# Split float32r probabilities and values, streamed q and k weights, and attended rows normalised on GpSimd, in a decoder layer on one core

## The chip, the cores and the metric

The kernel runs on one core of one Trainium2 chip. The metric is device time in microseconds. Before the change it was 2292.56 us, the median of 3 runs (2286.22 to 2292.59).

## What is computed

One decoder layer on x of 8 x 512 x 512 floats (B=8, S=512, D=512). It has three parts; the change lies in the first, the self-attention. It is done for each of the 8 batches:

```python
h = rmsnorm(layernorm(x)) * norm_w
q, k, v = h @ w_q, h @ w_k, h @ w_v            # 16 heads of 64
ll = where(causal, q @ k.T * 64**-0.5, -1e30)   # 512 x 512 a head
scores = h @ scorer_w                           # the 128 best tokens are attended to once more
lg = where(idx <= pos, q @ k[idx].T * 64**-0.5, -1e30)
attn = softmax(concat(ll, lg))
x1 = layernorm(x) + (attn_local @ v + attn_top @ v[idx]) @ w_out
```

A token among the 128 best counts twice, so the kernel doesn't gather: it multiplies the values and the sum's column by `twice` (1 or 2). Behind this part come a cross-attention with a router and a block on the routed tokens; both stay as they are.

## The kernel before

`self_attention` runs a loop over the 8 batches, and in it a plan (`attention_plan`) that every engine follows in the same order, each taking the steps that are its own. Semaphores order the engines among each other; on each engine the order is that of the plan.

A batch is one window of 512 tokens. TensorE first projects v (8 products of 128 tokens by 512 columns; each product is 12 float32r matmuls, as both operands are split into a high and a low float32r part and the low-low term is left out) and the first q and k. The 16 heads go in 8 pairs; a pair has five units u0 to u4, each of which fills a bank of 128 x 512 scores. u0 and u1 are the last 128 queries of either head against 512 keys, u2 and u3 the first 128 queries against 128 keys and the third 128 against 384, u4 the second 128 queries of both heads against 256 keys. So there are 40 units a batch (g or i in the plan, i = 5 p + u). At slot g the plan has, in this order:

- s(g): scores. TensorE adds q times the high part of k, q times the low part (`k_second`), and the causal mask as a bf16 product with the identity (L672 to L676). VectorE takes the negated maximum of each row (L543, L548), ScalarE the exponential into `probs` (L418).
- t(g-2): TensorE transposes the probabilities (L684), VectorE copies them from the bank to `probs_t` (L556).
- ot, only at g = 8, 13, ... (always a u3): TensorE transposes the attended rows of the pair before (L708), for which all five units of that pair must have been divided (`o_copied`). ScalarE copies them to `o_t` (L426).
- pv(g-3): TensorE multiplies the transposed probabilities by the values with a column of `twice` beside them (65 columns, f32, L699), VectorE takes the reciprocal of the sum and multiplies (L570, L571). TensorE's pv(i) needs `o_copied` of unit i-2.
- in u0 the projection of q for the next pair, in u2 that of k (L595 to L597). ScalarE makes the high parts (L405; L408 and L409, four copies of 64 partitions for k), VectorE the low parts (L532 in u1, L536 in u3). The scores of the next pair's u0 wait for both.
- single steps of the next batch: at g=5 its statistics (VectorE L439 to L443, then a chain on GpSimd L338 to L352 that ends in the normalised xb), at g=14 the dot product with the scorer, at g=18, 22, 24, 27, 29 the ranks that give `twice`; from g=40 on the transposes ht of the normalised tokens, between the last units.

The banks of t, ot, ht and score alternate between two: a transposition into a bank waits until the one two before it in this row has been read out (`ts_ready`, `ot_ready`). Score banks, `probs`, `probs_t` and output banks alternate in the same way. At the end of a batch TensorE multiplies `o_t` by `w_out` (out, L723) and VectorE adds the residual.

Ahead of the loop all weights are loaded and split whole: `w_q`, `w_k` and `w_v` come in six pieces of 1 MB through the two halves of `o_t`; ScalarE makes each high part (L381), VectorE each low part (`split`, L494), and pieces 2 to 5 (q and k) lie between the scorer's and the ranks' steps on VectorE. The first copy of v (L396, ScalarE) waits for `twice`.

## Time and profile before

| | |
|---|---|
| median of 3 runs | 2292.56 us |
| profiled execution, its own time | 2291.27 us |
| its span | 2289.5 us |
| mean granted clock of TensorE | 0.947 |
| busy: TensorE matmuls, weight loads | 2122.6 us (93%), 1653.9 us (72%) |
| busy: VectorE, ScalarE, GpSimd | 1340.6 (59%), 843.0 (37%), 429.6 us (19%) |
| pv, L699 (2560 matmul records) | 328.7 us busy, 271 ns each |
| copy of probabilities, VectorE L556 (320) | 217.6 us busy, 680 ns each |

Busy time counts an instruction from its start to its end, and matmuls overlap, so the mean of one is longer than its share of the engine; the distance between starts tells that. The attention's last VectorE operation starts at 1534.83 us, the cross part's first operations at 1538.03. Loads and matmuls of one f32 product are recorded as two passes each, those of float32r as one.

### The profile page before, as it was taken

What the parts mean: (1) busy time and instruction counts of PE and PEld (TensorE: products, weight loads), DVE (VectorE), ACT (ScalarE), POOL (GpSimd) and SP (SyncE); (2) the same over time, 40 slices, a digit from 0 to 9 for tenths busy, and PEclk for the clock granted to TensorE, in tenths of its full rate; (3) what the DMA queues carried; (4) which work ended last, traced back from release to release, by engine and by line L of the source; (5) the groups of instructions that cost most, each with busy time, mean ns of one, the idle gap of its engine ahead of it and who ended that gap; (6) DMA issues with size and microseconds to landing.
All of it is one profiled execution on the core that took longest, in us unless ns stands there. A gap on an engine that the chain in (4) does not pass through costs nothing. (4 is left out here: it accounts for less than half of the span.)

```text
span 2289.5 us, 35705 instructions
## 1 busy us (share of the span) xinstructions
PE 2122.6 (93%) x12029; PEld 1653.9 (72%) x12029; DVE 1340.6 (59%) x3146; ACT 843.0 (37%) x1541; POOL 429.6 (19%) x669
## 2 busy tenths in 40 slices
PE   3999999999999999999999999977899988978899
PEld 2886787688688688678768858846788887854543
DVE  5584376178177358537617817735887878645401
ACT  3442344244144144234424414415444444313210
POOL 2100000010010010000001001015776767420000
PEclk9999999999999999999999999998887979669899
DMA  5000000100100100000010010012023212150000
GB/s 197 1 1 34 28 1 15 47 1 1 61 1 1 61 1 1 33 29 1 15 47 1 1 61 1 1 57 62 27 68 129 62 57 72 38 201 1 0 0 19
DMA packets 47290, 82.33 MB, mean 36 GB/s; under 512 B 10196, under 2 KB 10196, under 8 KB 46602
## 3 DMA queue, kind: packets, MB, share of 16 engines
q1 hardware_dynamic: 46474, 77.95, 10.2%
q8 instruction: 103, 1.69, 0.3%
q0 software_dynamic: 640, 2.10, 0.2%
q14 instruction: 73, 0.60, 0.1%
HBM read 62.20 MB, written 17.83 MB: 35 GB/s over the span
## 5 line engine op out<-in xcount | busy, mean ns | idle before, releaser
L418 ACT ACTIVATE probs<-s_bank,nmax 128x512 f32<-128x512 f32 (+3 forms) x512 | 249.1, 525 | 364.0 <-DVE nmax L548 254.8
L699 PE MATMUL o_bank<-vals,probs_t 128*128 128x65 f32 x2560 | 328.7, 271 | 0.1
L699 PEld LDWEIGHTS o_bank<-vals,probs_t 128*128 128x128 f32 x2560 | 310.8, 192 | 14.9 <-DVE probs_t L556 12.9
L548 DVE TENSOR_REDUCE nmax<-s_bank 128x1 f32<-128x512 f32 (+2 forms) x384 | 184.2, 507 | 185.1 <-PE s_bank L676 182.4
L723 PE MATMUL pj_bank<-w_o,o_t 128*128 128x512 f32 x512 | 221.1, 592 | 0.0
L556 DVE COPY probs_t<-pt_bank 128x512 f32<-128x512 f32 x320 | 217.6, 680 | 0.1
L684 PE MATMUL pt_bank<-ident,probs 128*128 128x128 f32 x1280 | 194.0, 274 | 2.6 <-ACT o_t L426 2.6
L672 PE MATMUL s_bank<-k_twice,q_both 128*128 128x512 f32 (+3 forms) x512 | 189.9, 373 | 1.9 <-DVE k_second L536 1.9
L332 POOL TENSOR_TENSOR idle<-ones 128x4 f32<-128x4 f32 x41 | 10.0, 245 | 959.2 <-DMA probs<-in_x 957.1
L723 PEld LDWEIGHTS pj_bank<-w_o,o_t 128*128 128x128 f32 x512 | 96.6, 190 | 118.6 <-issue 118.6
L532 DVE SCALAR_TENSOR_TENSOR q_both<-pj_bank,q_both 64x512 fp32r<-64x512 f32 x128 | 88.1, 688 | 142.0 <-ACT q_both L405 139.3
L396 ACT ACTIVATE vals<-pj_bank,twice 128x512 f32<-128x512 f32 x64 | 43.9, 687 | 333.2 <-PE pj_bank L597 327.5
L674 PE MATMUL s_bank<-k_second,q_both 128*128 128x512 f32 (+3 forms) x512 | 163.9, 320 | 0.0
L1270 PEld LDWEIGHTS x_o_bank<-vx,p_t 77*128 77x128 f32 x1024 | 147.3, 222 | 16.9 <-issue 7.5
L1270 PE MATMUL x_o_bank<-vx,p_t 77*128 77x33 f32 x1024 | 141.9, 298 | 3.2 <-DVE att L1152 3.2
L684 PEld LDWEIGHTS pt_bank<-ident,probs 128*128 128x128 f32 x1280 | 135.5, 141 | 3.5 <-issue 3.5
L588 DVE TENSOR_TENSOR probs<-pj_bank,probs 128x512 f32<-128x512 f32 x32 | 22.1, 692 | 192.1 <-PE pj_bank L723 179.8
L595 PE MATMUL pj_bank<-wv_hi,ht_hi 128*128 128x512 f32 x256 | 104.6, 409 | 22.5 <-ACT vals L396 9.6
L1256 PE MATMUL e_bank<-qk_bd,xl_t 128*128 128x308 f32 x256 | 99.6, 522 | 23.4 <-DVE e L1134 22.7
L1033 POOL TENSOR_TENSOR e<-e,fill 128x616 f32<-128x616 f32 x64 | 95.3, 1490 | 123.1 <-DVE fill L1140 122.9
L676 PE MATMUL s_bank<-causal_b,ident_b 128*128 128x128 bf16 x512 | 117.8, 230 | 0.0
L405 ACT ACTIVATE q_both<-pj_bank 64x512 fp32r<-64x512 f32 x128 | 75.5, 590 | 88.7 <-PE pj_bank L597 88.0
(263 smaller groups left out, 4202.1 us busy)
## 6 DMA issues: line engine op xcount, KB each, us to landing
xb<-in_x SPq DMA_DIRECT2D x9, 1024.0 KB, 5.7
xt<-x SPq DMA_DIRECT2D x36, 256.0 KB, 3.0
probs<-in_x SPq DMA_DIRECT2D x32, 256.0 KB, 2.7
x<-probs SPq DMA_DIRECT2D x32, 256.0 KB, 2.0
am<-in_L_ffn_attention_mask SPq DMA_DIRECT2D x8, 1024.0 KB, 5.2
out<-x SPq DMA_DIRECT2D x32, 256.0 KB, 2.1
w_sb<-in_L_ffn_w SPq DMA_DIRECT2D x2, 4096.0 KB, 20.3
o_t<-in_L_attn_w_v SPq DMA_DIRECT2D x2, 1024.0 KB, 9.7
```

The lines of the kernel that those rows point to most:

```text
L418: ins = nc.scalar.activation(probs[:, i % 2, c0:c0 + nk], s_bank[i % 2][:, c0:c0 + nk], ACT.Exp, bias=nmax[:, i % 4, n:n + 1])
L548: ins = nc.vector.tensor_reduce(nmax[:, i % 4, n:n + 1], s_bank[i % 2][:, c0:c0 + nk], AX.X, ALU.max, negate=True)
L556: nc.vector.tensor_copy(probs_t[:, i % 2, :], pt_bank[slot][:, :]).then_inc(ts_ready, 1)
L595: nc.tensor.matmul(out, lhs_hi, rhs_hi, start=start, stop=False)
L672: nc.tensor.matmul(s_bank[slot][:, c0:c0 + nk], queries, k_twice[:, p % 2, h, 0:nk], start=True, stop=False)
L674: nc.tensor.matmul(s_bank[slot][:, c0:c0 + nk], queries, k_second[:, p % 2, h, 0:nk], start=False, stop=False)
L676: ins = nc.tensor.matmul(s_bank[slot][:, c0 + nk - P:c0 + nk], ident_b[:, :], causal_b[:, :], start=False, stop=True)
L684: ins = nc.tensor.transpose(pt_bank[slot][:, P * j:P * j + P], probs[:, i % 2, P * j:P * j + P], ident[:, :])
L699: ins = nc.tensor.matmul(o_bank[slot][:, o0:o0 + VW], probs_t[:, i % 2, c0 + P * kt:c0 + P * kt + P], vals[:, kt, 2 * p + h, :], start=(kt ...
L723: ins = nc.tensor.matmul(pj_bank[slot][:, :], o_t[:, c, P * i:P * i + P], w_o[:, c, :], start=(c == 0), stop=(c == NPAIR - 1))
L1256: ins = nc.tensor.matmul(e_bank[:, c, 0:CH * SK], xl_t[:, (i // 2) % 2, P * k:P * k + P], qk_bd[:, n.par, k].rearrange("p h k -> p (h k)") ...
L1270: ins = nc.tensor.matmul(o_bank[:, VX * h:VX * h + VX], p_t[:, i % 2, h // CH, P * (h % CH):P * (h % CH) + P], vx[:, n.par, 2 * CH * (i % ...
```

## The change

- pv: ScalarE copies the transposed probabilities to a float32r high part `pt_hi`, VectorE subtracts it from the bank for a low part `pt_lo`. The values are split too: columns 0 to 63 low, 64 to 127 high, and two columns of `twice`. TensorE multiplies `pt_hi` by all 130 columns and `pt_lo` by the 66 of the high part and the sum.
- the attended rows: ScalarE copies the bank to `o_part`, GpSimd adds low and high halves, raises the sum to the power -1 and multiplies. TensorE's pv(i) waits for that copy (`part_ready`) of unit i-2, ScalarE's copy for `o_copied` of unit i-2.
- q and k weights: no longer held whole. Each pair's 128 columns are loaded again in each batch into one of two buffers (SP, behind the projection that used the buffer); ScalarE makes the high part, GpSimd the low part, at the plan's new steps wq and wk (u3 and u4; in pair 0 at g = 1 to 4).
- ScalarE takes t(g-2) ahead of s(g). The causal mask and its identity are float32r instead of bf16. The self-attention's semaphores are cleared and a barrier follows it.

```diff
+WQ_AT = (1, *range(3, UNITS * (NPAIR - 1), UNITS))
+WK_AT = (2, *range(4, UNITS * (NPAIR - 1), UNITS))
...
+            def split_qk(b, n, i):
+                pl.wait_ge(wqk_hi_ready[n], b * NPAIR + i + 1)
+                nc.gpsimd.tensor_tensor(wqk_lo[:, i % 2, "qk".index(n)], wqk_raw[:, i % 2, "qk".index(n)],
+                                        wqk_hi[:, i % 2, "qk".index(n)].bitcast(F32),
+                                        ALU.subtract).then_inc(wqk_ready[n], 1)
...
+                    if kind == "pv":
+                        part = o_part[:, i % 2, 0:n, :]
+                        pl.wait_ge(part_ready, b * NU + i + 1)
+                        nc.gpsimd.tensor_tensor(part[:, :, 0:HD], part[:, :, 0:HD], part[:, :, HD:2 * HD],
+                                                ALU.add).then_inc(sum_ready, 1)
+                        step(nc.gpsimd.tensor_tensor(part[:, :, 2 * HD], part[:, :, 2 * HD], minus[:, 0:n], ALU.pow))
+                        pl.wait_ge(sum_ready, b * NU + i + 1)
+                        if u == 0 and p >= 1:
+                            pl.wait_ge(pt_ready, pt(b, ("ot", p - 1))[1])
+                        nc.gpsimd.tensor_tensor(dst, part[:, :, 0:HD],
+                                                part[:, :, 2 * HD:2 * HD + 1].broadcast_to((P, n, HD)),
+                                                ALU.mult).then_inc(o_copied, 1)
+                    if kind in ("wq", "wk"):
+                        split_qk(b, kind[1], i + 2)
...
+                    if kind == "t":
+                        slot, ready = pt(b, (kind, i))
+                        act.wait_ge(pt_ready, ready)
+                        if i >= 2:
+                            act.wait_ge(pv_ready, b * NU + i - 1)
+                        nc.scalar.copy(pt_hi[:, i % 2, :], pt_bank[slot][:, :]).then_inc(pt_hi_ready, 1)
+                    if kind == "pv":
+                        act.wait_ge(pv_ready, b * NU + i + 1)
+                        if i >= 2:
+                            act.wait_ge(o_copied, b * NU + i - 1)
+                        nc.scalar.copy(o_part[:, i % 2, 0:n, :],
+                                       o_bank[i % 2][:, 0:n * VW].rearrange("p (n v) -> p n v", n=n)
+                                       ).then_inc(part_ready, 1)
...
                     if kind == "t":
-                        nc.vector.tensor_copy(probs_t[:, i % 2, :], pt_bank[slot][:, :]).then_inc(ts_ready, 1)
-                    if kind == "pv":
-                        step(nc.vector.reciprocal(o_rden[:, i % 2, 0:n], src[:, :, HD]))
-                        nc.vector.tensor_tensor(dst, src[:, :, 0:HD],
-                                                o_rden[:, i % 2, 0:n].unsqueeze(2).broadcast_to((P, n, HD)),
-                                                ALU.mult).then_inc(o_copied, 1)
+                        dv.wait_ge(pt_hi_ready, b * NU + i + 1)
+                        nc.vector.tensor_tensor(pt_lo[:, i % 2, :], pt_bank[slot][:, :],
+                                                pt_hi[:, i % 2, :].bitcast(F32), ALU.subtract).then_inc(ts_ready, 1)
...
+                                nc.tensor.matmul(o_bank[slot][:, o0:o0 + VW], pt_hi[:, i % 2, keys],
+                                                 vals[:, kt, 2 * p + h, :], start=(kt == 0), stop=False)
+                                ins = nc.tensor.matmul(o_bank[slot][:, o0 + HD:o0 + VW], pt_lo[:, i % 2, keys],
+                                                       vals[:, kt, 2 * p + h, HD:VW], start=False, stop=last)
```

VectorE's splits of the q and k weights ahead of the loop (`split(2)` to `split(5)`) go, and it gains the low part of v, one operation for each product of v, with `v_ready` behind it.

## Rows read from the trace of the kernel before

**Rows 1.** Stretches: length, busy PE, PEld, DVE, ACT, POOL; clock, DMA share, GB/s.
```profile
50.00:55.00 5.00, 4.63 (x11) 3.67 (x12) 0.00 (x0) 0.90 (x2) 0.00 (x0) 0.52 0.05 16
500.00:550.00 50.00, 49.45 (x346) 42.62 (x345) 40.40 (x99) 23.94 (x46) 0.00 (x0) 1.00 0.00 1
```

**Rows 2.** Timeline of TensorE in batch 1: start, duration, operation, count.
```profile
269.73 0.22 PE L672 MATMUL s_bank<-k_twice,q_both 128*128 128x128 f32 x1
...
285.50 0.22 PE L672 MATMUL s_bank<-k_twice,q_both 128*128 128x128 f32 x1
...
286.66 0.60 PE L708 MATMUL pt_bank<-ident,o_norm 128*128 128x128 f32 x4
...
290.08 0.49 PE L672 MATMUL s_bank<-k_twice,q_both 128*128 128x512 f32 x1
...
291.32 1.11 PE L699 MATMUL o_bank<-vals,probs_t 128*128 128x65 f32 x8
292.23 0.48 PE L595 MATMUL pj_bank<-ht_hi,wq_hi 128*128 128x512 f32 x1
...
295.07 0.39 PE L672 MATMUL s_bank<-k_twice,q_both 128*128 128x512 f32 x1
```

**Rows 3.** Timeline of VectorE in the same stretch.
```profile
286.42 0.75 DVE L548 TENSOR_REDUCE nmax<-s_bank 128x1 f32<-128x128 f32 x2 [1.88 <-PE s_bank L676]
287.09 0.68 DVE L556 COPY probs_t<-pt_bank 128x512 f32<-128x512 f32 x1
...
288.42 0.23 DVE L571 TENSOR_TENSOR o_norm<-o_bank,o_rden 128x64 f32<-128x64 f32 x1
288.56 1.38 DVE L536 TENSOR_TENSOR k_second<-pj_bank,k_twice 64x512 fp32r<-64x512 f32 x2
...
290.58 0.68 DVE L556 COPY probs_t<-pt_bank 128x512 f32<-128x512 f32 x1
```

**Rows 4.** Groups by line and shape: busy us, mean ns; idle time before, its releasers.
```profile
L699 PEld LDWEIGHTS o_bank<-vals,probs_t 128*128 128x128 f32 x2560 | 310.8, 192 | 14.9 <-DVE probs_t L556 12.9
...
L674 PEld LDWEIGHTS s_bank<-k_second,q_both 128*128 128x128 f32 x512 | 97.7, 191 | 4.7
...
L676 PEld LDWEIGHTS s_bank<-causal_b,ident_b 128*128 128x128 bf16 x512 | 49.2, 96 | 59.8 <-issue 54.2
...
L1022 POOL TENSOR_TENSOR scales<-scales,x_half 128x1 f32<-128x1 f32 x32 | 20.5, 641 | 2.5
```

**Rows 5.** Timeline of the start: last split on VectorE, TensorE's wait.
```profile
47.08 2.28 DVE L494 TENSOR_TENSOR wk_lo<-o_t,wk_hi 128x2048 fp32r<-128x2048 f32 x1
...
50.37 0.80 PE L595 MATMUL pj_bank<-wv_hi,ht_hi 128*128 128x512 f32 x1 [9.65 <-ACT vals L396]
```

**Rows 6.** Timeline of ScalarE in the stretch of rows 2.
```profile
285.70 0.58 ACT L408 CAST k_twice<-pj_bank 64x512 fp32r<-64x512 f32 x1 [1.21 <-PE pj_bank L597]
...
288.08 0.84 ACT L418 ACTIVATE probs<-s_bank,nmax 128x128 f32<-128x128 f32 x2
288.81 0.59 ACT L426 COPY o_t<-pt_bank 128x512 f32<-128x512 f32 x1
```

**Rows 7.** Timeline of GpSimd: the statistics of the next batch.
```profile
279.83 0.20 POOL L338 TENSOR_TENSOR st<-mv,eps_ln 128x4 f32<-128x4 f32 x1 [53.61 <-DVE mv L443]
280.11 1.01 POOL L339 TENSOR_TENSOR st<-st,half 128x4 f32<-128x4 f32 x1
...
284.84 3.02 POOL L352 TENSOR_SCALAR xb<-xb,st 128x512 f32<-128x512 f32 x4
```

**Rows 8.** One line's instructions: ns min/median/max, first and last start.
```profile
L1042 POOL TENSOR_TENSOR x<-xt,att x64: 714/730/1179, 1578.4 to 1987.7; 128x256 f32<-128x256 f32 x64
```

**Rows 9.** Timeline of TensorE at the end of a batch.
```profile
386.99 1.11 PE L699 MATMUL o_bank<-vals,probs_t 128*128 128x65 f32 x8
387.94 0.61 PE L623 MATMUL pt_bank<-ident,xb 128*128 128x128 f32 x4
389.09 0.65 PE L708 MATMUL pt_bank<-ident,o_norm 128*128 128x128 f32 x4 [0.55 <-DVE o_norm L571]
```

More of the change, by code:

```diff
@@ L42 @@
 NU = NPAIR * UNITS
-VW = HD + 1
+VW = 2 * HD + 2
 class Tally:
@@ L116, in attention_plan, with transposes_first @@
             plan.append(("ht", g - NU))
+        if g in WQ_AT:
+            plan.append(("wq", WQ_AT.index(g)))
+        if g in WK_AT:
+            plan.append(("wk", WK_AT.index(g)))
     plan += [("out", t) for t in range(TT)]
     return plan
+def transposes_first(plan):
+    order = list(plan)
+    for n in range(len(order) - 1):
+        if order[n][0] == "s" and order[n + 1][0] == "t":
+            order[n], order[n + 1] = order[n + 1], order[n]
+    return order
 def bank_index(plan, kinds):
@@ L192, in self_attention @@
         pj_ready, row_copied = sem("pj_ready"), sem("row_copied")
-        v_ready, v_sum_ready, qk_hi, qk_lo = sem("v_ready"), sem("v_sum_ready"), sem("qk_hi"), sem("qk_lo")
+        v_hi_ready, v_ready, v_sum_ready, qk_hi, qk_lo = (
+            sem(n) for n in ("v_hi_ready", "v_ready", "v_sum_ready", "qk_hi", "qk_lo"))
+        wqk_in = {n: [sem(f"w{n}_in{i}") for i in range(2)] for n in "qk"}
+        wqk_hi_ready = {n: sem(f"w{n}_hi_ready") for n in "qk"}
+        wqk_ready = {n: sem(f"w{n}_ready") for n in "qk"}
         s_ready = sem("s_ready")
@@ L272, in _, with next_weights @@
             sp.wait_ge(sw_out, 16)
+            def next_weights(b):
+                for i in range(NPAIR):
+                    for n in "qk":
+                        sp.wait_ge(pj_ready, pj(b, (n, i))[1])
+                        load_qk(n, (i + 2) % NPAIR)
             def results(b):
@@ L299, in _ @@
                 sp.wait_ge(half_done, 16 * B * TT // 2 + 1)
+            for n in "qk":
+                for half_in in wqk_in[n]:
+                    sp.wait_ge(half_in, 16 * (B * NPAIR // 2 + 1))
         @block.gpsimd
@@ L353, in stats @@
                                             ALU.mult, ALU.add).then_inc(h_ready, 1)
+            def split_qk(b, n, i):
[3 more added lines that the diff above has]
+                                        ALU.subtract).then_inc(wqk_ready[n], 1)
             stats(0)
-            with pl.Fori(0, B) as b, done.loop(b, 14 + TT, B):
+            for i in range(2):
+                for n in "qk":
+                    split_qk(0, n, i)
+            with pl.Fori(0, B) as b, done.loop(b, 14 + TT + NU, B):
                 for r in range(2):
```

176 lines of the change are left out of this document (100 added, 76 removed).

## The prediction

> **What bounds the kernel now.** I read the page first, then the stretches, then the timelines of one stretch engine by engine. The page says that TensorE works through nearly all of the span and that the self-attention fills the first 1535 us of it; only that part is edited. The stretches show a steady one: TensorE is busy 49.45 of 50 us, VectorE 40.40, ScalarE 23.94, GpSimd 0.00, at full clock [rows 1]. So GpSimd is free and VectorE is the second busiest, but a busy TensorE only says that it sets the pace, not that nobody makes it wait. For that I read the timeline of a pair's stretch [rows 2]. A pair of heads has five units u0 to u4; in each slot TensorE does s (scores), t (transposes of the unit two slots earlier) and pv (of three slots earlier), and in u0 and u2 a q or k projection. From s(u3) at 285.50 to the q projection at 292.23 there is no projection: 6.73 us. Nearly all of it is back to back; the starts of s(u0) and pv(u2) alone are late, and they stand right behind VectorE's rows: k_second ends at 289.94 and s(u0) starts at 290.08, the copy of unit u2 ends at 291.26 and pv(u2) starts at 291.32 [rows 2, 3]. TensorE's own work is therefore the floor, and what waits cost is read in this stretch.
>
> **TensorE's work stays.** pv has 8 f32 passes a unit now, and 8 float32r matmuls after (4 high of 130 columns, 4 low of 66). The weight load is 192 ns a pass in f32 and 191 ns in float32r [rows 4], and the eight passes of pv(u2) take 0.91 us, 291.32 to 292.23 [rows 2], 0.114 each; as the loads are alike, I let the load set the pace of both. I take 0 for the swap; ends: -0.04 us a pass (2560 passes, -105 us) if float32r loads could hide, +0 otherwise, near the row of equal loads. The causal matmul loses its short bf16 load (96 against 191 ns, 512 times: at most +49 us). But the loader stands idle for 59.8 us in all before these loads, 54.2 of it at issue, and for 4.7 before as many float32r loads [rows 4]: at most -55 us. The two are alike; I take 0.
>
> **Start.** Four splits of q and k weights leave VectorE, 2.29 us each, the last at 47.08 [rows 5]; the v block on TensorE waits 9.65 us for work behind them, until 50.37 [rows 5]. 50.37 - 4 x 2.29 + 0.75 for the new low part of v = 42.0: -8.4 us. The long idle time had also let the granted clock fall: it is 0.52 from 50 to 55 us, where eleven matmuls run at half speed [rows 1]. About 2 us come back if the idle time is only 1.5 us. Start: **-10 us**. The small loads and splits that come instead (ScalarE 4 x 0.59, GpSimd 4 x 1.2) lie beside the first v block.
>
> **The prices of what is moved.** ScalarE: copy of the transposed probabilities 0.59, as the 128x512 copy at 288.81 [rows 6]; copy of the attended rows 0.3 (130 columns) or 0.4 (260), under that 0.59; split of weights 0.6 for q and k, once a pair. VectorE: the copy of 0.68 becomes a subtraction of about the same length (k_second: 1.38 for two [rows 3]); reciprocal and multiplication leave. GpSimd has no row of these shapes: 4 elements of a two-input operation take 0.20 [rows 7], 256 take 0.73 in the median and 1.18 at most [rows 8], so 64 or 128 take 0.4 or 0.5; a power takes 0.64 for one element [rows 4] and 1.01 for four [rows 7], so 0.6 or 0.7; dependent steps stand 0.08 apart (280.03 to 280.11 [rows 7]). One unit: 0.4+0.6+0.4+0.1 = **1.5** (u0, u1) or 0.5+0.7+0.5+0.16 = **1.86** (u2 to u4); bounds 1.0 and 2.6. A weight split of 512 columns: 1.2 (0.73 to 1.46). The Trainium skill (GPSIMD Engine Reference, Engine selection) speaks against this move: it puts a two-input elementwise operation on GpSimd at about twice VectorE's time. By its ratio of 1.96 and the 0.23 us of VectorE's 64-element multiplication [rows 3] such an operation would take 0.45 instead of 0.4, an estimate from that page, and the sum below would be some 2 us higher.
>
> **The walk through a pair (0 = start of s(u3)).** Check on before: k copies on ScalarE end at 2.56, k_second runs 3.06 to 4.44, s(u0) starts 4.58, pv(u2) 5.82, q 6.73 [rows 2, 3, 6]. After: the copies of k still end at 2.56, and only then ScalarE makes the high part of u1, to 3.15; its low part on VectorE 3.2 to 3.9. k_second slides behind it, 3.9 to 5.3. t(u2) on TensorE uses the bank of t(u1), free at 3.9 instead of 2.3: it starts at 3.95, 0.8 us after s(u4) is through. pv(u1) follows without a gap; s(u0) waits for k_second until 5.35. On ScalarE come exponential 0.73, o_t 0.59, attended rows 0.3, weight split 0.6, and the high part of u2 ends at 6.0; its low part at 6.7; pv(u2) starts at 6.75 and q at 7.65. That is **+0.93 us a pair**; the slots with q and k projections (2.84 us each, 292.23 to 295.07 [rows 2]) take up the rest. Four pairs of a batch (stretches behind k of pairs 3 to 6) go like this: +3.7 us. Bounds 0.3 and 1.6 a pair.
>
> **The queue behind the statistics.** GpSimd does the next batch's statistics at g=5, a chain of steps from 279.83 to 287.86, 8.03 us [rows 7]. Now it does nothing else; after the change pv(3) and pv(4) of pair 0 are queued behind it. The transposes ot(0) on TensorE (g=8) need all five units of pair 0. Counted from s(u3) of pair 0 (269.73), VectorE's statistics are ready at 10.1 now and, with the first stretch 1.4 us longer (one more weight split lies in it) and the low parts, at 12.7; GpSimd ends them at 20.7, pv(3) and pv(4) at 24.5. ot(0) starts at 16.93 now [rows 2], and TensorE, 2 us later by these two, would reach it at 18.9: it stands for 5.6 us, and what is queued behind it (pv(5), s, t) with it. In the stretch behind, everyone has caught up, -0.5. Sum **+7.1 us a batch**; bounds 3 (GpSimd at its cheap prices) and 9. TensorE idles long enough there that its clock may fall: it was 0.52 after the 9.65 us at the start, full after the waits of under 1 us elsewhere [rows 1, 5]. Cost 0 or about 2.2 us; I take **+1.1**.
>
> **The pair without projections and the tail.** Behind k of the last pair no projection gives time back: the walk continued loses 1.25 us up to the next u2. Then ot(6) waits for pv of unit 34: ScalarE has it copied 1.1 us behind its end, GpSimd adds 1.86, while only s and t lie between: **+1.8**. At the end ot(7) starts at 389.09, 1.15 us after pv(39) is through and the ht transposes behind it begin (387.94 [rows 9]); after, the ScalarE copy (0.45) and GpSimd with the unit before still in its queue (2.4) come between: **+1.7**. VectorE's relief takes away about -0.5 a batch, where score and ranks made TensorE wait. The longer way of v through VectorE (0.75 us) lies within the next projection of 2.84 us and costs nothing; uncovered it would be 8 x 0.75 us a batch.
>
> **Sum.** A batch: 7.1 + 1.1 + 3.7 + 1.25 + 1.8 + 1.7 - 0.5 = 16.1; eight: +129. Start -10. The added clearing of semaphores and barrier between attention and cross part: +1 (0 to 5). Total +120. The profiled execution took 2291.27 us (span 2289.5), 1.3 under the median of the runs, so **2411 us**, by either.
>
> **Rivals.**
> 1. The statistics queue costs little (GpSimd's steps at 0.2 to 0.3 us, the stats reached earlier), pairs cost as walked: 129 - 8 x 7 = 73, less 10: 2354. For: GpSimd's rows for these shapes are missing. Against: even at 1.0 us a unit, pv(4) ends later than TensorE gets to ot(0).
> 2. Faster. The float32r passes of pv run under the row that I went by: the loads hide and a pass takes some 0.07 us. It decides from about 0.05 us less a pass, since 2560 passes must pay for 120 us. At 0.07 with half of the walked waits: 2291 - 105 + 65 - 10 = 2241; at half the effect 2285. For: a float32r matmul is one pass, an f32 one two. Against: the load rows of 191 and 192 ns.
> 3. Slower still: GpSimd shares its way to memory with VectorE's two-input operations, and a unit takes 2.6 us; then it is later than TensorE in every pair's ot, about 1.5 us each, and in the tail: +80, 2490. For: the 256-element operation takes up to 1.18 us in the cross part [rows 8], where both are busy. Against: the VectorE operations here read one operand from a bank of TensorE's.
>
> **Chances.** Forecast (2370 to 2450) 0.54, rival 1 (2320 to 2370) 0.20, rival 3 0.10, rival 2 0.12, all covered and no change 0.04. 0.3% (7 us) is about what a measurement can tell here: faster 0.12, same 0.04, slower 0.84. The range leaves out rival 2, no change and the upper end of rival 3: 2320 to 2475.
>
> **What would show it.** Right: in the changed trace, per batch one wait of 4 to 7 us of TensorE at the ot transposes of pair 0, released by GpSimd; s(u3) to q about 7.6 us in later pairs, with t(u2) waiting for the low part; pv at 0.9 us for eight; ot(7) about 3 us after pv(39). VectorE under 1300 us busy, ScalarE about 1200, GpSimd about 1000. Wrong: pv clearly under 0.8 us, no wait at ot, or stretches that keep 6.7 us; then TensorE's floor moved or the queues cover more than walked.

## The result and the profile after

The changed kernel takes 2467.16 us in the median (2454.63 to 2476.08, 4 runs), the kernel before 2290.5 us beside it: ratio 1.077, 95% interval 1.0717 to 1.0823. It is slower, as forecast, and the time lies within the range given (2320 to 2475 us), but above the 2370 to 2450 us that had the largest chance, and 56 us above the 2411 us predicted. The profiled execution of the changed kernel took 2454.63 us (span 2452.9), 163 us more than the profiled one of before, which took 2291.27 us (span 2289.5).

Busy times of the changed kernel, from the page's first part and its row of the granted clock in 40 slices; below them its span and mean granted clock:

```profile
PE 2204.3 (90%) x12029; PEld 1761.0 (72%) x12029; DVE 1311.1 (53%) x2566; ACT 1139.9 (46%) x2309; POOL 1048.3 (43%) x1762
...
PEclk9899989999899998999999989998888788858999
...
core 0: 2452.9 us, clock 0.919
```

GpSimd went from 429.6 to 1048.3 us, ScalarE from 843.0 to 1139.9, VectorE from 1340.6 to 1311.1, and no engine but TensorE is near its span. The new thing is the clock: 0.919 in the mean, where before had 0.947. At full clock a share of 1 is 2.4 GHz and at half 1.2 GHz, so a mean of 0.919 over 2452.9 us is 2 x 0.081 x 2452.9 = 397 us at half clock; before it was 2 x 0.053 x 2289.5 = 243 us, nearly all behind the attention. The change added some 150 us of half clock.

Where it begins is seen in the first batch. The same engine's rows in stretches of the changed kernel (start:end, length, busy time and count of TensorE, its weight loads, VectorE, ScalarE, GpSimd, then the granted clock):

```profile
50.00:55.00 5.00, 5.00 (x23) 4.14 (x23) 1.50 (x2) 1.38 (x2) 0.00 (x0) 1.00 0.01 3
...
88.00:99.00 11.00, 7.05 (x50) 6.33 (x48) 6.90 (x14) 7.20 (x15) 9.66 (x22) 0.98 0.16 48
99.00:109.00 10.00, 9.62 (x45) 9.43 (x45) 2.65 (x4) 4.66 (x10) 5.04 (x9) 0.50 0.01 2
109.00:114.00 5.00, 5.00 (x18) 4.01 (x18) 0.11 (x1) 0.73 (x2) 1.53 (x3) 0.67 0.00 0
150.00:200.00 50.00, 48.02 (x333) 42.82 (x331) 35.83 (x67) 37.32 (x81) 26.90 (x50) 1.00 0.11 33
```

The half clock of the start is gone: 1.00 in 50 to 55 us, against 0.52 [rows 1]. From 99 to 109 us the clock is 0.50. TensorE's timeline and GpSimd's tell why (start, duration, engine, line, operands, count; in brackets the idle time just before and who ended it). First TensorE:

```profile
99.38 1.11 PE L806 MATMUL pt_bank<-ident,o_norm 128*128 128x128 f32 x4 [4.33 <-POOL o_norm L441]
100.14 0.46 PE L796 MATMUL o_bank<-vals,pt_hi 128*128 128x130 f32 x1
...
109.12 0.77 PE L690 MATMUL pj_bank<-ht_hi,wqk_hi 128*128 128x512 f32 x1
...
113.45 0.40 PE L767 MATMUL s_bank<-k_twice,q_both 128*128 128x512 f32 x1
```

Then GpSimd:

```profile
88.16 0.20 POOL L389 TENSOR_TENSOR st<-mv,eps_ln 128x4 f32<-128x4 f32 x1 [0.48 <-DVE mv L550]
...
93.18 3.02 POOL L403 TENSOR_SCALAR xb<-xb,st 128x512 f32<-128x512 f32 x4
96.17 0.46 POOL L435 TENSOR_TENSOR o_part<-o_part 128x128 f32<-128x128 f32 x1
96.58 0.71 POOL L437 TENSOR_TENSOR o_part<-o_part,minus 128x2 f32<-128x2 f32 x1
97.36 0.40 POOL L441 TENSOR_TENSOR o_norm<-o_part 128x128 f32<-128x128 f32 x1
...
98.92 0.40 POOL L441 TENSOR_TENSOR o_norm<-o_part 128x128 f32<-128x128 f32 x1
```

GpSimd does the next batch's statistics from 88.16 to 96.2, 8.0 us as in [rows 7], then the units 3 and 4 of pair 0; only with the last, at 99.3, may TensorE do ot(0). It has stood for 4.33 us, and behind that wait the next 10 us run at half clock: a pv of eight matmuls starts at 100.14 and the next s at 101.85, 1.71 us where it is 0.89 elsewhere. The q projection that starts at 109.12 takes 4.33 us instead of 2.84, and during it the clock comes back.

Not every batch goes like this. TensorE at ot(0) in the second batch and in the fourth:

```profile
308.35 1.11 PE L806 MATMUL pt_bank<-ident,o_norm 128*128 128x128 f32 x4 [4.29 <-POOL o_norm L441]
...
722.21 0.66 PE L806 MATMUL pt_bank<-ident,o_norm 128*128 128x128 f32 x4 [1.13 <-POOL o_norm L441]
```

In batches 1, 2, 5 and 7 the wait is 4.27 to 4.33 us, and 13.7 us at half clock go with it. In batches 3, 4, 6 and 8 the clock has been at half for 6.8 us one stretch earlier (in the fourth from 706.2 to 713.1 us), so TensorE comes to ot(0) later, waits 1.11 to 1.58 us, and no half clock follows. The waits ahead of that earlier fall (1.12 and 0.29 us, between k(1) and q(2)) are the same in all eight batches; why the clock falls there in only four of them is not shown.

A later pair, at full clock, is where the walk of the prediction can be checked. Timeline of all engines, changed kernel, from s(u3) to the next q:

```profile
173.94 0.22 PE L767 MATMUL s_bank<-k_twice,q_both 128*128 128x128 f32 x1
...
175.91 0.58 ACT L500 CAST k_twice<-pj_bank 64x512 fp32r<-64x512 f32 x1
...
176.51 0.59 ACT L517 CAST pt_hi<-pt_bank 128x512 fp32r<-128x512 f32 x1
...
177.13 0.69 DVE L667 TENSOR_TENSOR pt_lo<-pt_bank,pt_hi 128x512 fp32r<-128x512 f32 x1 [1.50 <-ACT pt_hi L517]
...
177.74 1.38 DVE L649 TENSOR_TENSOR k_second<-pj_bank,k_twice 64x512 fp32r<-64x512 f32 x2
...
179.25 0.50 PE L767 MATMUL s_bank<-k_twice,q_both 128*128 128x512 f32 x1
...
180.62 0.33 PE L796 MATMUL o_bank<-vals,pt_hi 128*128 128x130 f32 x1
...
181.54 0.47 PE L690 MATMUL pj_bank<-ht_hi,wqk_hi 128*128 128x512 f32 x1
```

173.94 to 181.54 is 7.60 us, against 6.73 [rows 2]. The last copy of k ends at 176.49, only then comes pt_hi, then pt_lo, then k_second to 179.12, then s(u0): the chain as it was walked. k_second takes 1.38 us as before, and the copies end 2.55 us after s(u3), where it was 2.56 [rows 3, 6].

The groups of instructions that were priced blind (changed kernel, by form; busy time and mean ns of one, then idle time before):

```profile
L796 PEld LDWEIGHTS o_bank<-vals,pt_hi 128*128 128x128 f32 x1280 | 260.3, 203 | 45.1 <-DVE pt_lo L667 45.0
L771 PEld LDWEIGHTS s_bank<-causal_r,ident_r 128*128 128x128 f32 x512 | 98.9, 193 | 5.5
L435 POOL TENSOR_TENSOR o_part<-o_part 128x128 f32<-128x128 f32 x192 | 88.3, 460 | 192.4 <-ACT o_part L523 191.6
L437 POOL TENSOR_TENSOR o_part<-o_part,minus 128x2 f32<-128x2 f32 x192 | 143.5, 748 | 0.0
L441 POOL TENSOR_TENSOR o_norm<-o_part 128x128 f32<-128x128 f32 x192 | 76.7, 400 | 15.1
```

And the end of the first batch, TensorE, which answers to [rows 9]:

```profile
214.47 0.66 PE L718 MATMUL pt_bank<-ident,xb 128*128 128x128 f32 x4
216.85 0.65 PE L806 MATMUL pt_bank<-ident,o_norm 128*128 128x128 f32 x4 [1.73 <-POOL o_norm L441]
```

### Where the 163 us are

TensorE's timeline was cut at its projections: for each batch the stretch from the first matmul behind one 12-matmul projection to the start of the next. This table is worked out from it, as means over batches 2 to 8, in us (e2 and e9 are experiments below). In the changed kernel the 11.02 us of k(2) to q(3) are a mean of 15.4 us in batches 2, 5 and 7 and 7.6 to 8.1 us in the others.

| stretch | before | changed | e2 | e9 |
|---|---|---|---|---|
| k(1) to q(2) | 6.27 | 8.58 | 8.32 | 7.09 |
| k(2) to q(3), with ot(0) | 6.73 | 11.02 | 7.60 | 6.96 |
| k(3) to q(4) | 6.73 | 7.60 | 7.60 | 6.96 |
| q(4) to k(4), behind the dot products | 3.98 | 5.61 | 5.61 | 6.19 |
| k(4) to q(5), with the score row | 7.33 | 8.27 | 8.26 | 7.72 |
| k(5) to q(6) and k(6) to q(7), together | 13.72 | 15.20 | 15.20 | 13.92 |
| k(7) to the output projection | 22.86 | 29.11 | 28.05 | 26.74 |
| the 14 projections themselves | 39.80 | 41.41 | 40.29 | 40.17 |
| output projection, to the next v (in batch 8 to the first matmul of the cross part) | 30.15 | 31.51 | 31.21 | 30.31 |

The differences of the first two columns sum to 20.7 us a batch, and smaller ones make it 21.1. Eight of these are 169 us; the first batch, 22.9 us longer, adds 1.8, and the start gives back 7.5 (q(0) starts at 55.96 instead of 63.45). Behind the attention's last matmul the two kernels take the same, 755.0 and 754.8 us. The last two rows do the same matmuls in both kernels, so their 1.6 and 1.4 us are put down to the clock.

### The profile page after: what moved, and what is told of

It reads as the page before. It is cut to its first block and busy times, and to the rows that moved or that the text cites. A ratio compares the mean times of both kernels' runs of the same rounds, so it can differ in the third digit from the quotient of the medians.

```text
span 2452.9 us, 38352 instructions
## 1 busy us (share of the span) xinstructions
PE 2204.3 (90%) x12029; PEld 1761.0 (72%) x12029; DVE 1311.1 (53%) x2566; ACT 1139.9 (46%) x2309; POOL 1048.3 (43%) x1762
## 5 line engine op out<-in xcount | busy, mean ns | idle before, releaser
L796 PE MATMUL o_bank<-vals,pt_hi 128*128 128x130 f32 x1280 | 335.5, 322 | 24.9 <-DVE pt_lo L667 18.8
L667 DVE TENSOR_TENSOR pt_lo<-pt_bank,pt_hi 128x512 fp32r<-128x512 f32 x320 | 220.9, 690 | 177.0 <-ACT pt_hi L517 173.7
L798 PE MATMUL o_bank<-vals,pt_lo 128*128 128x66 f32 x1280 | 307.7, 255 | 0.0
L796 PEld LDWEIGHTS o_bank<-vals,pt_hi 128*128 128x128 f32 x1280 | 260.3, 203 | 45.1 <-DVE pt_lo L667 45.0
L798 PEld LDWEIGHTS o_bank<-vals,pt_lo 128*128 128x128 f32 x1280 | 261.1, 204 | 0.0
L437 POOL TENSOR_TENSOR o_part<-o_part,minus 128x2 f32<-128x2 f32 (+1 forms) x320 | 218.7, 683 | 0.0
L690 PE MATMUL pj_bank<-ht_hi,wqk_hi 128*128 128x512 f32 x512 | 215.9, 422 | 0.0
L517 ACT CAST pt_hi<-pt_bank 128x512 fp32r<-128x512 f32 x320 | 190.3, 595 | 54.2 <-PE pt_bank L779 50.9
L691 PE MATMUL pj_bank<-ht_hi,wqk_lo 128*128 128x512 f32 x512 | 205.2, 401 | 0.0
L692 PE MATMUL pj_bank<-ht_lo,wqk_hi 128*128 128x512 f32 x512 | 205.1, 401 | 0.0
```

What stands on the lines that cost most here:

```text
L437: step(nc.gpsimd.tensor_tensor(part[:, :, 2 * HD], part[:, :, 2 * HD], minus[:, 0:n], ALU.pow))
L517: nc.scalar.copy(pt_hi[:, i % 2, :], pt_bank[slot][:, :]).then_inc(pt_hi_ready, 1)
L667: nc.vector.tensor_tensor(pt_lo[:, i % 2, :], pt_bank[slot][:, :], pt_hi[:, i % 2, :].bitcast(F32), ALU.subtract).then_inc(ts_ready, 1)
L690: nc.tensor.matmul(out, lhs_hi, rhs_hi, start=start, stop=False)
L691: nc.tensor.matmul(out, lhs_lo, rhs_hi, start=False, stop=False)
L692: return nc.tensor.matmul(out, lhs_hi, rhs_lo, start=False, stop=stop)
```

## The experiments

Each starts from the changed kernel unless it says otherwise; an edit shifts the line numbers by a few. Mean granted clocks are those of the profiled execution.

### e1: attended rows on VectorE

```diff
-                        nc.gpsimd.tensor_tensor(part[:, :, 0:HD], part[:, :, 0:HD], part[:, :, HD:2 * HD],
-                                                ALU.add).then_inc(sum_ready, 1)
-                        step(nc.gpsimd.tensor_tensor(part[:, :, 2 * HD], part[:, :, 2 * HD], minus[:, 0:n], ALU.pow))
...
-                        nc.gpsimd.tensor_tensor(dst, part[:, :, 0:HD],
...
+                        nc.vector.tensor_tensor(part[:, :, 0:HD], part[:, :, 0:HD], part[:, :, HD:2 * HD],
+                                                ALU.add).then_inc(sum_ready, 1)
+                        step(nc.vector.reciprocal(part[:, :, 2 * HD], part[:, :, 2 * HD]))
...
+                        nc.vector.tensor_tensor(dst, part[:, :, 0:HD],
...
```

> One part of the change is undone: ScalarE still copies the attended rows to o_part, but the addition, the reciprocal and the multiplication run on VectorE, at the place that the plan gives them, and GpSimd has none of them. Theory (the queue behind the row statistics, the 1.6 us of a unit on GpSimd and the half clock that follows its wait): the waits of 4.3 us at ot(0), some 1.5 us at ot(6) and 1.2 us at the tail go (-56 us in 8 batches), and most of the 157 us of half clock inside the attention with them (-40 to -55 us), while VectorE pays some 0.6 to 0.9 us a unit, mostly beside TensorE: 2340 to 2390 us. Rival (what is late is the copies on ScalarE and the chain through VectorE, GpSimd only shows it): 2440 us or more, since both stay and VectorE gets more to do.

2597.58 us (ratio to before 1.1347, 1.1313 to 1.1381), 130 us slower than the changed kernel; clock 0.882. The theory missed by 200 us, and the rival's sign was right. The waits at ot that end on the units fall to 10.2 us in all (48.6 in the changed kernel), much as expected, but VectorE, which takes its work in order, now waits for ScalarE's copy in nearly every unit (waits of e1: engine, what, who; us in total, times, longest):

```profile
DVE o_part L660 <- ACT o_part L503: 141.9, 308, 1.8
...
PE s_bank L767 <- DVE k_second L629: 60.0, 48, 1.4
```

308 times it stands 0.46 us, and k_second, queued behind, makes TensorE wait 1.25 us in 48 pairs. The pairs' stretches become 9.3 to 10.5 us, and in them the clock falls: in e1's stretches 84 to 92, 104 to 112 and 124 to 132 us it is granted 0.57, 0.58 and 0.61.

```profile
84.00:92.00 8.00, 7.86 (x28) 6.45 (x27) 5.86 (x19) 3.01 (x8) 2.36 (x3) 0.57 0.00 0
```

So taking the units back from GpSimd does not give the time back: with a ScalarE copy ahead of the division, the engine that waits for that copy must not be the one on the pair's chain.

### e2: statistics ahead of the units

```diff
+    plan = [("v", i) for i in range(2 * TT - 2)] + [("stats", 0), ("q", 0), ("q_lo", 0), ("k", 0), ("k_lo", 0)]
...
-        if g == 5:
-            plan.append(("stats", 0))
```

> The row statistics of the next batch move from behind g = 5 of the plan to behind the sixth of the v projections, so that GpSimd's 8 us of small steps and normalisation lie ahead of the first unit. Nothing else changes. Theory (queue behind the statistics, then half clock): the 4.3 us at ot(0) go in each batch (-35 us), and the 13.7 to 17.1 us at half clock that begin with that wait go too (half of some 100 us, -40 us or less, since the clock also falls at the tail): 2390 to 2425 us. Rival (GpSimd's 1.6 us a unit is itself too slow and the queue only shows it): ot(0) still waits over 3 us, 2450 to 2470 us.

2410.97 us (1.0536, 1.0513 to 1.0558), 56 us less; clock 0.936. The theory held, though it took the 4.3 us for every batch and they stand in four. The stretch with ot(0) falls from 11.02 to 7.60 us and is like its neighbours. What is left of the waits at ot is the small ones and the last pairs', 32 in all and none over 1.7 us:

```profile
PE pt_bank L804 <- POOL o_norm L439: 27.0, 32, 1.7
```

In the changed kernel this row reads 48.6 us, 40 times, 4.3 at most. The profiled executions are 46 us apart (2454.63 and 2408.58). Of these 8 x 3.4 = 27 lie in that stretch and 8 x 1.1 = 9 in the tail; the projections and the output gave 8 x 1.4 = 11, and these do the same work, so they are put down to the clock.

### e3: the same wait, with TensorE kept busy

```diff
+                        if i == 0:
+                            for n in range(16):
+                                nc.tensor.matmul(pt_bank[slot][:, :], ident_r[:, :], ht_hi[:, n % DC, :],
+                                                 start=True, stop=True)
                         pe.wait_ge(o_copied, b * NU + UNITS * (i + 1))
```

> The wait at ot(0) stays, but ahead of it TensorE runs 16 float32r products of 512 columns into the bank that ot(0) will fill (some 3.5 us at full clock), so that it is busy for most of the 4.3 us instead of idle. Theory (much of the loss is the clock, which fell during the idle wait and stayed at half for up to 17 us): the granted clock stays full through g = 8 of the plan and the time falls by 25 to 45 us, to 2420 to 2445 us, although work is added. Rival (the wait itself is the loss, the clock is not): no gain, 2460 to 2480 us.

2442.65 us (1.0647, 1.0615 to 1.0679), 24.5 us less, at the edge of what the theory gave; clock 0.930. The wait at ot(0) remains (TensorE comes to ot(0) no earlier), 16 products were added in every batch, and the kernel became faster. In the first batch the stretch that had 0.50 is at full clock:

```profile
98.50:109.00 10.50, 9.89 (x66) 8.60 (x65) 4.74 (x7) 6.05 (x14) 8.19 (x16) 1.00 0.01 2
```

No batch has half clock behind ot(0) any more. The clock still fell in the tails, which this edit leaves alone, and in four batches between k(1) and q(2).

### e5: the k copies divided

```diff
+                    if kind == "k":
...
+                        dv.wait_ge(pj_ready, ready)
+                        nc.vector.tensor_copy(k_twice[head_rows(0), i % 2, 1, :], pj_bank[slot][head_rows(1), :]
+                                              ).then_inc(k_across, 1)
...
+                        dv.wait_ge(k_half, b * NPAIR + i + 1)
+                        nc.vector.tensor_tensor(k_second[own, i % 2, 0, :], pj_bank[slot][own, :],
+                                                k_twice[own, i % 2, 0, :].bitcast(F32), ALU.subtract)
```

> At each k projection the two halves of partitions are worked on at the same time: VectorE makes one of ScalarE's four copies and the first half of k_second while ScalarE is in the other half, so the chain of four copies, pt_hi, pt_lo and two k_second is about 1.2 us shorter. Theory (that chain sets the stretch from s(u3) to the next q, which went from 6.73 to 7.60 us): the stretch goes back to 6.4 to 6.8 us, -0.8 to -1.2 us in some 6 pairs of 8 batches, 2405 to 2430 us. Rival (something else, the units on GpSimd or the copies of attended rows, is late next): the stretch stays near 7.6 us, 2455 to 2470 us.

2509.01 us (1.0958, 1.0936 to 1.0981), 42 us slower; clock 0.900. Neither case. Where no ranking step lies in the pair the stretch fell as the theory said (k(3) to q(4) 7.60 to 6.97, k(1) to q(2) to 7.10), but in the two pairs with ranking it rose to 9.7 and 10.1. The edit had put VectorE's new step ahead of the ranking, which stands between k and the next s in the plan. VectorE in e5, behind the projection of k(6):

```profile
180.65 0.68 DVE L651 TENSOR_TENSOR k_second<-pj_bank,k_twice 64x512 fp32r<-64x512 f32 x1 [0.51 <-ACT k_twice L504]
181.25 0.73 DVE L581 TENSOR_SCALAR_CACHE_REDUCE junk<-row_s,score 128x512 bf16<-128x512 f32 x1
...
182.91 0.75 DVE L675 TENSOR_REDUCE nmax<-s_bank 128x1 f32<-128x128 f32 x2
183.58 0.68 DVE L681 TENSOR_TENSOR pt_lo<-pt_bank,pt_hi 128x512 fp32r<-128x512 f32 x1
```

The 1.6 us of ranking, which in the changed kernel begin while TensorE is still in the k projection, now begin at 181.25, 2.0 us after it, and nmax, pt_lo and the second k_second are queued behind them. That part was a fault of the edit, not of either theory. Another part is the queue and the clock again: with k(1) to q(2) at 7.10 us and no fall of the clock there, TensorE comes to ot(0) early in every batch, waits 4.3 us there in all eight instead of four, and k(2) to q(3) takes 15.2 us in the mean instead of 11.02, the 14 projections 45.2 instead of 41.4.

### e6: statistics ahead, and k divided behind the ranking

```diff
+                    if kind == "s" and i % UNITS == 3 and i // UNITS + 1 < NPAIR:
+                        k_across_and_half(b, i // UNITS + 1)
```

> The changed kernel with the statistics moved into the v phase, and with the work at each k projection divided by halves of the partitions between ScalarE and VectorE, this time behind the ranking steps. Theory (the stretch of a pair is set by the chain of copies and splits; put ahead of the ranking it had been undone by it): stretches of 6.9 to 7.1 us instead of 7.6 in all pairs, 0.6 to 1.0 us in 6 pairs of 8 batches, and less half clock: 2360 to 2385 us. Rival (moving work to VectorE there costs what it gains): 2405 to 2420 us, as with the statistics alone.

2402.57 us (1.0497, 1.0478 to 1.0517): 8 us under e2 and 18 above the theory's upper end; clock 0.914, lower than e2's 0.936. The stretches are what the theory said (6.97 us in all ordinary pairs, some 4 us a batch less than in e2), but the tail took it back: k(7) to the output rose from 28.05 to 31.87 us. Stretch of e6 behind the wait at ot(6):

```profile
194.00:213.00 19.00, 17.71 (x83) 16.86 (x82) 5.02 (x7) 7.92 (x16) 8.64 (x19) 0.50 0.09 28
```

### e9: e6 with the tail's waits filled

```diff
+                        if i >= NPAIR - 2:
+                            for n in range(8):
+                                nc.tensor.matmul(pt_bank[slot][:, :], ident_r[:, :], wv_hi[:, n % DC, 0:512],
+                                                 start=True, stop=True)
                         pe.wait_ge(o_copied, b * NU + UNITS * (i + 1))
```

> The kernel of e6 (statistics in the v phase, k work divided), and at ot(6) and ot(7) TensorE runs 8 float32r products of 512 columns into the bank that the transposes will fill, where it would wait some 1.8 us. Theory (the gain in the pairs was lost because the clock fell at the wait of ot(6), and the last pair, the tail and part of the output projection ran at half): the half clock of 17 to 20.5 us at each batch's end goes, 31 to 32.6 us from the last k projection to the output become some 27 us, 2355 to 2375 us. Rival (the tail is long because GpSimd's units and ScalarE's copies are late there): 2395 to 2410 us.

2348.82 us (1.0254, 1.0238 to 1.0270), 54 us less than e6 and a little better than the theory; clock 0.945. The tail is 26.74 us in every batch, and in e9 the stretch that ends with the first output projection is at full clock:

```profile
190.00:208.00 18.00, 17.35 (x130) 15.36 (x128) 8.51 (x14) 11.04 (x26) 13.59 (x29) 1.00 0.10 32
```

With its GpSimd queue cleared, its chain shortened and its waits filled the changed design is still 2.5% behind.

### e4: the streamed weights alone, on the kernel before

```diff
-        w_hi = {n: sb(f"w{n}_hi", [P, DC, H * HD], F32R) for n in "qkv"}
+        wqk_hi = sb("wqk_hi", [P, 2, 2, DC, P], F32R)
...
+                    if kind in ("wq", "wk"):
+                        split_qk(b, kind[1], i + 2)
```

> The kernel before with one part of the change alone: the weights of q and k are read pair by pair and split on ScalarE and GpSimd beside the attention; probabilities, values and the division stay as before. Theory (the change gained 7.5 us at the start, where v no longer stands among the splits of q and k, and the reads and splits beside the attention cost nothing): 2280 to 2286 us, ratio 0.9955 to 0.9985. Rival (the ScalarE copies of 0.65 us and GpSimd's subtractions of 1.3 us are late in some pairs, which in the changed kernel could not be told from the rest): 2295 us or more, with a batch longer than 186.1 us.

2292.15 us (1.0005, 0.9995 to 1.0015): between the two. The batch is longer, as the rival had it, but neither ScalarE nor the splits are late. The start did gain: the first output projection begins at 198.2 instead of 204.5 us. But a batch takes 187.1 instead of 186.1, and that is one stretch, q(4) to k(4), 3.98 to 4.99 (k(3) to q(4) grew by 0.26 and k(5) to q(6) shrank by as much). It lies behind the dot products of the next batch. VectorE and GpSimd in e4:

```profile
114.71 0.69 DVE L508 CUSTOM_DVE_ANT_0 junk<-xb,row_s 128x512 bf16<-128x512 f32 x1
...
115.45 1.70 DVE L508 CUSTOM_DVE_ANT_0 junk<-xb,row_s 128x512 bf16<-128x512 f32 x1
...
115.31 1.29 POOL L392 TENSOR_TENSOR wqk_lo<-wqk_raw,wqk_hi 128x512 fp32r<-128x512 f32 x1 [1.19 <-ACT wqk_hi L428]
```

Of four equal products the one that meets GpSimd's subtraction takes 1.70 us instead of 0.69. It ends at 117.15, about where the end of the subtraction, 116.60, and its own 0.69 us would put it. In sum the streamed weights alone cost nothing that these runs can tell: what the changed kernel loses does not come from them alone.

### e10: that split moved off the dot products

```diff
-WK_AT = (2, *range(4, UNITS * (NPAIR - 1), UNITS))
+WK_AT = (2, 4, 9, 16, *range(19, UNITS * (NPAIR - 1), UNITS))
```

> The streamed weights alone, with one split of k (copy on ScalarE, subtraction on GpSimd) moved from g = 14 of the plan, where VectorE runs the dot products of the next batch, to g = 16. Theory (VectorE's product of two operands stood at 1.70 us instead of 0.69 us beside GpSimd's subtraction of 1.29 us, and that 1.0 us in each batch took the 6 us that the start had gained): a batch of 186.1 us instead of 187.1 us, 2281 to 2286 us. Rival (the long product has another cause, such as the read of xb): 2289 to 2294 us, one product still at 1.70 us.

2281.53 us (0.9968, 0.9956 to 0.9980): faster than before by 0.2 to 0.4%, and with e11 the fastest of all. The stretch is back at 3.98 us, a batch at 186.1, and the products take 0.69 us each. The theory held. VectorE in e10, the product that had met the subtraction and the next one, then a ranking step:

```profile
114.57 0.69 DVE L508 CUSTOM_DVE_ANT_0 junk<-xb,row_s 128x512 bf16<-128x512 f32 x1
...
115.30 0.69 DVE L508 CUSTOM_DVE_ANT_0 junk<-xb,row_s 128x512 bf16<-128x512 f32 x1
...
147.77 1.75 DVE L528 SCALAR_TENSOR_TENSOR junk<-row_s,score,before 128x512 bf16<-128x512 f32 x1
```

That ranking step takes 0.75 us when it is alone. In e4 and in e10 it takes 1.74 to 1.75 us in 16 of its 36 times, each of them beside a GpSimd split, but the stretches of those pairs did not grow.

### e7 and e11: k divided, on the kernel before

Both take e6's edit, which divides k in all eight pairs; e11 leaves pairs 0, 1 and 4 out of it (its line in place of e7's):

```diff
+K_ACROSS = (2, 3, 5, 6, 7)
...
-                    if kind == "s" and i % UNITS == 3 and i // UNITS + 1 < NPAIR:
+                    if kind == "s" and i % UNITS == 3 and i // UNITS + 1 in K_ACROSS:
```

> The streamed weights alone on the kernel before, and at each k projection VectorE makes one of ScalarE's four copies and the first half of k_second while ScalarE is in the other half of the partitions (after the ranking steps of the same place, not before them). Theory (in the kernel before, too, the stretch from s(u3) to the next q of 6.73 us holds some 0.4 us of waits on that chain, as the pair without a load on it, 6.27 us, suggests): 0.3 to 0.45 us in 6 pairs of 8 batches on top of the streaming, 2257 to 2272 us. Rival (the chain is not what these waits end on): no better than the streaming alone, 2280 to 2290 us.

> The same move of one split, and the k projections of pairs 2, 3, 5, 6 and 7 divided by halves of the partitions between ScalarE and VectorE (pairs 1 and 4, which it had made 0.4 us longer, as before). Theory: the stretches keep what each was better at, some 0.4 us a batch on top of the move: 2276 to 2284 us. Rival (the division gains nothing once the ranking steps are not late): as the move alone, 2281 to 2286 us.

e7 is e4 with e6's division of k: 2286.52 us (0.9985, 0.9975 to 0.9995). e11 is e10 with it in five pairs: 2281.68 us (0.9966, 0.9952 to 0.9979). The theory of e7 fell: the ordinary stretches went from 6.73 to 6.69 us only, that from k(3) to q(4) from 6.99 to 6.69, and two others rose by 0.4. In the kernel before, the chain through k is not what those waits end on. What e7 did gain on e4 (a batch of 186.25 us instead of 187.09) lies elsewhere: with the k of pair 0 divided, v(0) to q(1) takes 28.16 us instead of 29.31. e11 left that pair out, so this gain together with the moved split was not measured. e11 keeps the better stretches, a batch of 185.6 us instead of e10's 186.1, and is not faster: its attention ends 4 us earlier, but the parts behind its last matmul took 757 us in its profiled execution and 752 in e10's, though the code there is the same but for two more semaphores to clear; over all profiled executions these parts took 752 to 759 us. Whether those 0.5 us a batch are worth anything is not settled.

### e8 and e12: a wait alone, and the same wait filled

e8, on e4's kernel:

```diff
+                        for r in range(2):
+                            ins = nc.gpsimd.tensor_tensor(late_t[:, 1 + r, :], late_t[:, 0, :], late_t[:, 0, :], ALU.add)
+                        ins.then_inc(late, 1)
...
+                        if i == 0:
+                            pe.wait_ge(late, b + 2)
```

e12 adds, ahead of that wait:

```diff
+                            for n in range(14):
+                                nc.tensor.matmul(pt_bank[slot][:, :], ht_hi[:, 0, 0:P], ht_hi[:, n % DC, :],
+                                                 start=True, stop=True)
```

> The kernel with the streamed weights alone (no split of probabilities, no units on GpSimd), and one wait added: ahead of ot(0) TensorE waits for GpSimd to end the next batch's statistics and two additions of 128x512 after them, which lands some 4 us after ot(0) could start. Theory of the clock: the wait of about 4 us in each batch drops the granted clock to half, and it stays there until a projection has run, so that a batch costs 4 us and 4 to 8 us more: 2340 to 2385 us, with a stretch of half clock behind each wait. Rival (the clock fell in the changed kernel for other reasons, such as its many small products): the wait costs itself alone, 2310 to 2325 us, and no half clock.

> The kernel of e8, streamed weights and one added wait of some 3.3 us at ot(0), and in that wait TensorE runs 14 float32r products of 512 columns into the bank that ot(0) will fill. Theory of the clock: no half clock behind the wait, the wait costs itself alone, 2315 to 2325 us, though TensorE does 14 products more in each batch. Rival (the half clock had another cause): 2345 to 2355 us as without them.

e8: 2351.25 us (1.0262, 1.0242 to 1.0282), 59 us above e4, clock 0.931 against 0.947. e12: 2321.75 us (1.0140, 1.0124 to 1.0155), 30 us above e4, clock 0.950. Both as the theory of the clock said. TensorE's wait in e8's first batch:

```profile
95.65 0.66 PE L772 MATMUL pt_bank<-ident,o_norm 128*128 128x128 f32 x4 [3.10 <-POOL late_t L415]
```

The stretches of that wait and behind it in e8's first batch, then, as the third line, behind it in its second; below them e12's first batch:

```profile
92.00:96.00 4.00, 0.90 (x9) 0.66 (x8) 1.35 (x3) 2.59 (x6) 3.59 (x5) 1.00 0.22 66
96.00:100.00 4.00, 4.00 (x24) 3.81 (x23) 2.12 (x5) 1.10 (x2) 1.27 (x1) 0.57 0.00 0
...
285.00:300.00 15.00, 12.79 (x57) 11.51 (x58) 5.25 (x13) 4.30 (x9) 4.70 (x5) 0.66 0.01 3
```

```profile
96.00:100.00 4.00, 4.00 (x34) 3.46 (x32) 1.78 (x5) 1.10 (x2) 1.74 (x2) 1.00 0.02 4
```

The wait costs 3.4 us a batch, as e12 shows: its batch is 190.45 us against 187.09. The clock behind it costs 4.3 more, as e8 shows with 194.7. In e8 there are no splits of probabilities and no units on GpSimd, so a wait of 3.1 us alone is enough. The length of what follows varies: in the first batch the clock is full again from 100 us on, in the second 0.66 over 15 us is 2 x 0.34 x 15 = 10 us of half clock.

## Why the prediction was right in sign and short in size

By its steps, for one batch of the changed kernel:

- **TensorE's work stays: right.** Loads of 203 ns for float32r in pv and 193 for the causal matmul, against 192 and 191 [rows 4]; eight matmuls of pv take 0.89 to 0.92 us. Rival 2 fell with that: no pass got cheaper. (At half its effect its own terms give 2291 - 52 + 65 - 10 = 2294 us, not 2285.)
- **Start, -10: measured -7.5.** The idle time and its half clock went as foreseen. What was missed is 2.9 us on the way: the score's transposes start at 34.70 us instead of 31.84, because the dot products run beside GpSimd's four splits and take 1.62 to 1.70 us each. "Lie beside the first v block" was wrong: the splits run ahead of that block, which starts at 35.47, and TensorE waits for the scores behind them.

```profile
27.58 1.70 DVE L559 CUSTOM_DVE_ANT_0 junk<-xb,row_s 128x512 bf16<-128x512 f32 x1
...
27.47 6.27 POOL L409 TENSOR_TENSOR wqk_lo<-wqk_raw,wqk_hi 128x512 fp32r<-128x512 f32 x4 [6.15 <-ACT wqk_hi L465]
```

- **Prices on GpSimd: some 15% high.** A unit of u2 to u4 takes 0.46 + 0.75 + 0.40 = 1.61 us without its gaps, against 0.5 + 0.7 + 0.5 + 0.16; in its rows the steps touch (96.17 to 97.76 for one unit, 1.59 against 1.86). The 64-element multiplication takes 0.29 us, under the 0.4 taken and the 0.45 estimated beside it.
- **Walk through a pair, +0.93: right, +0.87.** The four pairs that it was counted for took 3.3 us more (0.87, 0.93, 0.61 and 0.87) instead of 3.7. What it left out is the stretch behind the dot products, q(4) to k(4): +1.6. Of this e4 shows 1.0 for a GpSimd split beside a dot product.
- **Queue behind the statistics, +7.1: the mechanism right, the size not.** TensorE waits 4.3 us instead of 5.6, and in four batches instead of each. With TensorE kept at full clock k(2) to q(3) is about 10.87 us (e3, batches 1, 2, 3 and 5), 4.1 more than before; with the 1.85 of k(1) to q(2) at full clock (8.12 against 6.27), which the 7.1 held too, that is 6.0, the units being cheaper than priced. e2 shows that the wait goes when the queue does.
- **Clock, +1.1: the step that failed.** It was priced as one fall of 2.2 us with even odds, at ot(0) alone. The table's last two rows alone give 3.0 us a batch, the tail another 2.2 (26.92 at full clock, 29.11 in the mean), and some 0.9 lie in other stretches: about 6.1. It falls at ot(0), at the waits of ot(6) and ot(7), and in four batches already between k(1) and q(2). e3, e9 and e12 show that it is the clock: adding matmuls to a wait made the kernel faster by 24.5, 54 and 29.5 us.
- **Last pair, ot(6), tail, +4.75: right, 4.1 at full clock** (26.92 against 22.86).
- **VectorE's relief, -0.5: about half of it came.** Of the stretches with the score row and the ranking only k(5) to q(6) rose less than the others, 6.99 to 7.60, where k(6) to q(7) went from 6.73 to 7.60. These 0.3 us are counted with the four pairs above.

Predicted 16.1, measured 21.1: +5.0 clock, +1.6 the stretch behind the dot products, +0.5 relief, -0.4 the four pairs, -1.1 statistics, -0.7 tail make the 5 us. Eight times that is 40 us; with 1.8 more in the first batch, 2.5 of the start, -0.8 behind the attention (0.2 came where 1 was taken), and 12.5 us between the profiled execution and the median it is the 56. The terms that were too high gave back 2.2 us a batch, 18 us in all; without them the time would have left the range, whose upper end is 8 us away, so that it held is in part luck.

The four runs of the changed kernel spread over 0.9%, where the four of before spread over 0.3%. The clock falls in some batches and not in others, which could do that, but the mean clocks of the four (0.919, 0.918, 0.911 and 0.923) do not follow their times (2454.63, 2463.59, 2476.08 and 2470.74 us): the cause of the spread is not shown.

Rival 1 was half right (the queue is cheaper than priced), and what it saved was more than eaten by the clock. Rival 3 had a true mechanism in the wrong place: the units did not take 2.6 us, but VectorE's operations that read both operands from tiles that are not banks do take longer beside GpSimd's splits, in the dot products (1.62 to 1.70 us) and in the ranking (1.75, e4 and e10).

One thing stays open: what share of the changed design's last 2.5% (e9) is the copies on ScalarE and what the split of probabilities itself; no run has the one without the other. The causal mask in float32r and ScalarE's new order were not undone alone either.

## What to carry to other kernels

Price a new wait of TensorE twice, once by its length and once by the half-clock run that may follow it; if the wait can't be removed, matmuls into a bank that will be overwritten anyway cost less here than the half clock did (e3, e9, e12). Before a helper engine gets units that another engine waits for, look for the longest thing already in its queue and move that first (e2 gave back 56 us by one line of the plan). And when work is "beside" other work, check it engine by engine: the streamed weights were free for TensorE and ScalarE, and cost VectorE about what they had gained (8 x 1.0 us against 6.3 at the start), until one split was moved (e10).

## What the runs showed of the hardware that was not expected

- **One wait, long half clock.** A wait of 3.1 us (e8) or 4.33 us is followed by 3.4 to 13.7 us at 1.2 GHz, while TensorE is busy nearly all the time: 9.62 of 10 us from 99 to 109 in the changed kernel, at 0.50. Transposes, scores and pv ran there; the level rose again during a projection in the changed kernel, and in e8's first batch without one. The clock fell behind shorter waits too: in e1 TensorE waits 1.12 us up to 81.29 and 1.07 up to 83.44, and from 84 to 92 us the clock is 0.57. But 1.12 and 0.29 us between k(1) and q(2) in the changed kernel were followed by half clock in four batches of eight. The Trainium skill (TensorE: Matmul & The Clock Gate, section HAM oscillation — how this bites in real kernels) describes a kernel whose waits drop the clock each time anew, and advises to group its matmuls ahead of the wait so that the clock stays up. e8 and e12 agree that a wait drops the clock and that matmuls in it keep the clock up, with 59 and 30 us for the same wait.
- **A product of 0.69 us becomes 1.70 us** beside one GpSimd operation of 1.29 us (e4), and 0.69 again when that is moved (e10). The Trainium skill (SBUF — State Buffer, section SBUF: two separate sides) says that a VectorE operation with two inputs in SBUF and a GpSimd operation that reads SBUF exclude each other for the whole instruction; the rows agree. VectorE's splits and copies out of a bank, 0.69 us each in e4 and in the changed kernel, were not slowed.
- **Float32r weights load no faster than f32 ones**, 203 ns in the mean (half-clock loads among them) against 192 in pv, and eight float32r matmuls of 130 and 66 columns took as long as eight f32 passes of 65 (0.89 to 0.92 us against 0.91).
